# Key transposes of four heads at a time, rows doubled at read-out, in a cross-attention and expert-FFN kernel

## The reference

```
q = (layernorm(x) @ Wq + bq) in heads of 16
k = concat(side @ Wk + bk, ctx);  v = concat(side @ Wv + bv, ctx)
x = x + softmax(q k^T / 4) v @ Wp + bp
z = layernorm(x)
cw = softmax(z @ w_router) * softmax(z @ w_gating / 0.1);  cw /= sum(cw) + 1e-9
x = x + sum over 8 experts of cw[e] * ((silu(z @ w_gate[e]) * (z @ w_up[e])) @ w_down[e])
```

## Time and profile before

| what | value |
|---|---|
| median of 3 runs | 2790.26 us (2788.6 to 2790.9) |
| the profiled execution | 2790.06 us, of which its span is 2788.0 us |
| TensorE, VectorE, GpSimd, ScalarE busy | 98%, 79%, 65%, 61% of the span |
| granted TensorE clock, mean | 0.994 |
| HBM traffic | 89 GB/s over the span |

### The profile page before, as it was taken

The page is one execution under the profiler, slowest core; times in us unless marked ns, Lnnn a source line. Parts: engine busy times, 40 slices in busy tenths (PEclk is TensorE's granted clock), DMA queues, the critical chain, the costliest instruction groups (busy, mean ns, idle before and its releaser), DMA issues.

```text
span 2788.0 us, 47546 instructions
## 1 busy us (share of the span) xinstructions
PE 2723.0 (98%) x16416; PEld 2224.3 (80%) x16416; DVE 2189.3 (79%) x3254; ACT 1695.2 (61%) x3241; POOL 1813.8 (65%) x1886
## 2 busy tenths in 40 slices
PE   7789999999999999999999999999999999999998
PEld 5578878888887878878788787887878788888887
DVE  7877788778888788777787788877878778776665
ACT  7766666665666666566665666656666665544443
POOL 6766676666666667666676666766666666655554
PEclk9999999999999999999999999999999999999999
DMA  2113232332322323323222322323323233333332
GB/s 69 36 60 99 80 92 96 91 103 77 98 91 92 102 76 95 95 92 98 80 92 91 100 90 88 96 84 110 91 77 99 76 103 92 95 106 112 106 105 83
DMA packets 251275, 252.27 MB, mean 90 GB/s; under 512 B 15904, under 2 KB 242848, under 8 KB 251040
## 3 DMA queue, kind: packets, MB, share of 16 engines
q1 hardware_dynamic: 251040, 249.25, 28.8%
HBM read 240.66 MB, written 8.52 MB: 89 GB/s over the span
## 4 chain that ended last, share of the span: by engine, by line
PE 87%; DVE 7%; ACT 3%; issue 3%; POOL 1%; DMA 0%; POOLq 0%; ACTq 0%; DVEq 0%
PE ps_s L660 23%; PE ps_t L660 23%; PE ps_o L694 23%; PE ps_s L753 4%; PE ps_t L763 3%; PE ps_m L549 3%; PE ps_a L735 2%; PE ps_a L737 2%; DVE h_lo L949 2%; DVE negmax L1139 1%; PE ps_m L597 1%; PE ps_m L557 1%; DVE hf L944 1%; ACT h_hi L782 1%; DVE hf L937 1%
## 5 line engine op out<-in xcount | busy, mean ns | idle before, releaser
L949 DVE TENSOR_TENSOR h_lo<-hf,h_hi 128x512 fp32r<-128x512 f32 x512 | 506.0, 988 | 231.6 <-ACT h_hi L782 221.4
L782 ACT ACTIVATE h_hi<-hf 128x512 fp32r<-128x512 f32 x512 | 323.9, 633 | 510.6 <-DVE hf L944 510.6
L937 DVE SCALAR_TENSOR_TENSOR hf<-hf,ps_s 128x512 f32<-128x512 f32 x512 | 349.8, 683 | 278.0 <-ACT hf L777 275.2
L777 ACT ACTIVATE hf<-ps_s 128x512 f32<-128x512 f32 x512 | 305.6, 597 | 312.4 <-PE ps_s L660 204.5
L1170 POOL TENSOR_TENSOR wg_lo<-stage_w,wg_hi 128x512 fp32r<-128x512 f32 x256 | 340.0, 1328 | 224.1 <-ACT wg_hi L789 223.9
L1235 POOL TENSOR_TENSOR Pt_lo<-Pt 128x512 f16<-128x512 f32 x256 | 312.3, 1220 | 149.0 <-ACT Pt L916 148.5
L694 PE MATMUL ps_o<-h_hi,wd_hi 128*128 128x512 f32 x1024 | 399.9, 390 | 0.9 <-DVE h_lo L949 0.9
L694 PE MATMUL ps_o<-h_lo,wd_hi 128*128 128x512 f32 x1024 | 400.1, 391 | 0.0
L694 PE MATMUL ps_o<-h_hi,wd_lo 128*128 128x512 f32 x1024 | 398.5, 389 | 0.0
L1170 POOL TENSOR_TENSOR wd_lo<-stage_w,wd_hi 128x512 fp32r<-128x512 f32 x256 | 332.5, 1299 | 82.5 <-ACT wd_hi L789 82.4
L916 ACT ACTIVATE Pt<-ps_t 128x512 f32<-128x512 f32 x512 | 304.5, 596 | 124.1 <-PE ps_t L763 120.3
(11 more groups left out here) (193 smaller groups left out, 5117.0 us busy)
## 6 DMA issues: line engine op xcount, KB each, us to landing
stage_w<-in_L_ffn_w_gate_dram SPq DMA_DIRECT2D x256, 256.0 KB, 2.7
stage_w<-in_L_ffn_w_up_dram SPq DMA_DIRECT2D x256, 256.0 KB, 2.8
stage_w<-in_L_ffn_w_down_dram SPq DMA_DIRECT2D x256, 256.0 KB, 2.7
...
```

The source lines that it names most:

```text
L777: act.activation(hf[:], ps_g[:], ACT.Tanh, scale=0.5).then_inc(tanh_done, 1)
L782: act.activation(h_hi[f % FC][:], hf[:], ACT.Copy).then_inc(hh_done, 1)
L937: dve.scalar_tensor_tensor(out=hf[:], in0=hf[:], scalar=1.0, in1=ps_g[:], op0=ALU.add, op1=ALU.mult).then_inc(gate_done, 1)
L949: dve.tensor_tensor(h_lo[f % FC][:], hf[:], h_hi[f % FC][:].bitcast(F32), ALU.subtract).then_inc(hl_done, 1)
```

## The change

For batches 3 to 15 (`by_quad`) the eight items `kT` become four items `kQ`, at steps 12, 19 and 27 of the turn before and step 0 of its own. `kstack` is used as `qkeys`, with two slots a head (low, high), so that one transpose takes four heads: 4 x 2 x 16 = 128 columns. The doubling of the rows and the ones are made afterwards: `keys_out` on ScalarE copies, for each pair of heads, four blocks of 32 partitions (each head's low and high rows, twice) from PSUM to `KTs`, the first pair in the item's own program and the second in the next one; VectorE then sets 3 rows of ones in each head, two memsets of 3x512 in the program after each read-out. TensorE's score block waits for the ones as well. ScalarE's copies into the stack are half as wide.

The router arithmetic goes over programs 19 to 22, `cwT` to step 24, `d_cw` to step 25, and the reading back of `cwb` three (and two) steps later. `o`, `kv`, `xT` and `y` move one to two steps earlier, and so do the stack copies (from programs 12, 13 to 10, 11).

```diff
-                self.qs_at, self.ks_at, self.ms_at = (10, 8, 5) if b == -1 else (18, 12, 13)
+                self.qs_at, self.ks_at, self.ms_at = (10, 8, 5) if b == -1 else (18, 10, 11)
...
-                 (6, "qq", 2, 0), (8, "o", 0, -1), (9, "kv", 0, 1), (10, "qq", 3, 0), (11, "kv", 1, 1), (13, "xT", 0, 1),
+                 (6, "qq", 2, 0), (7, "o", 0, -1), (8, "kv", 0, 1), (9, "kv", 1, 1), (10, "qq", 3, 0), (11, "xT", 0, 1),
...
-                 (20, "kT", 1, 1), (21, "cwT", 0, -1), (22, "qq", 6, 0), (23, "y", 0, 0), (24, "y", 1, 0), (25, "kT", 2, 1),
-                 (26, "qq", 7, 0), (27, "kT", 3, 1), (28, "kT", 4, 1), (30, "qq", 0, 1)]
+                 (20, "kT", 1, 1), (21, "y", 0, 0), (22, "qq", 6, 0), (23, "y", 1, 0), (24, "cwT", 0, -1), (25, "kT", 2, 1),
+                 (26, "qq", 7, 0), (27, "kT", 3, 1), (28, "kT", 4, 1), (30, "qq", 0, 1),
+                 (0, "kQ", 3, 0), (12, "kQ", 0, 1), (19, "kQ", 1, 1), (27, "kQ", 2, 1)]
...
+            def keys_out(turn, ps, pair, d):
+
+                turn.wait(act, t_ps, d - 1, 4 * pair + 4)
+                for h in range(2):
+                    for part in range(2):
+                        src = 2 * HD * (pair % 2 * 2 + h)
+                        dst = HS * h + 2 * HD * part
+                        act.activation(KTs[dst:dst + 2 * HD, pair, :], ps[src:src + 2 * HD, :], ACT.Copy).then_inc(kT_done, 1)
...
+                    if name == "kQ":
+                        turn.wait(act, kT_ps, d, 2 * k + 2)
+                        keys_out(turn, ps, 2 * k, d)
+                    if keys_next:
+                        keys_out(turn, bank(keys_next[3]), 2 * keys_next[1] + 1, keys_next[2])
+                    keys_next = items[turn.b, step] if name == "kQ" else None
...
+                if step == 20:
                     turn.wait(dve, lsum_done, -1, 1)
                     dve.scalar_tensor_tensor(out=css[:], in0=lsum[:, :, 0], scalar=CW_EPS, in1=lsum[:, :, 1],
...
-                if step == 20:
+                if step == 21:
                     turn.wait(dve, csum_done, -1, 2)
...
+                if step == 22:
                     turn.wait(dve, crec_done, -1, 1)
...
+                            for h in range(2):
+                                ones = slice(HS * h + 2 * HD, HS * h + 2 * HD + 3)
+                                dve.memset(KTs[ones, pair, :].bitcast(F32), 1.0).then_inc(ones_done, 1)
```

More of the change, by code:

```diff
@@ L57, in bass_xattn_moe_ffn_kernel @@
     DVE_LOW = (1, 3, 5, 7)
+    QUADS = PAIRS // 2
+    FIRST_QUAD = 3
     SCALE = float(HD) ** -0.5
@@ L290, in q_ahead, with by_quad, keys_done @@
             return (k + 2) % PAIRS, d + (k + 2) // PAIRS
+        def by_quad(b):
+            return b >= FIRST_QUAD
+        def keys_done(b, pairs):
+            late = max(b - FIRST_QUAD, 0)
+            return (b - late) * PAIRS + late * 2 * QT * PAIRS + pairs * (2 * QT if by_quad(b) else 1)
         def released(b, name, k, d):
             turn = Turn(b)
+            if name in ("kT", "kQ"):
+                if not turn.has(d) or by_quad(b + d) != (name == "kQ"):
+                    return []
+                return [(kT_done, keys_done(b + d, 2 * k + 2 if name == "kQ" else k + 1))]
             if name == "y":
@@ L468, in body @@
                         eng.dma_start(x1_v[:, bass.ds((turn.b - 1) * QT, QT), :], X1[:]).then_inc(x1_out.sem, 16)
-                    if step == 22 and turn.has(-1):
+                    if step == 25 and turn.has(-1):
                         turn.wait(eng, cwT_done, -1, 1)
@@ L599, in do_misc @@
                     mm.then_inc(kT_ps.sem, 1)
+                elif name == "kQ":
+                    if k == 0:
+                        for count in (ks_h, ks_l, ms_h, ms_l):
+                            turn.wait(pe, count, 1, 1)
+                    for t in range(KC):
+                        mm = pe.transpose(ps[:, t * P:(t + 1) * P].bitcast(F32R), quad_block(t, k), ident_r[:])
+                    mm.then_inc(kT_ps.sem, 2)
                 elif name == "qq":
@@ L748, in body @@
                         if i % 4 == 0:
-                            turn.wait(pe, kT_done, d, h // 2 + 1)
+                            pe.wait_ge(kT_done, keys_done(turn.b + d, h // 2 + 1))
+                            if by_quad(turn.b + d):
+                                pe.wait_ge(ones_done, 2 * ((turn.b + d - FIRST_QUAD) * PAIRS + h // 2 + 1))
                             turn.wait(pe, qT_done, d, 2 * (h // 2) + 2)
@@ L842, in body @@
                         turn.wait(act, kT_ps, 0, PAIRS)
-                        act.activation(slots(kstack, 0, 0, 4, 3), heads_twice(KF), ACT.Copy).then_inc(ks_h.sem, 1)
+                        if by_quad(turn.b + 1):
+                            act.activation(qkeys[:, 0:QT * H, 1, :], heads(KF), ACT.Copy).then_inc(ks_h.sem, 1)
+                        else:
+                            act.activation(slots(kstack, 0, 0, 4, 3), heads_twice(KF), ACT.Copy).then_inc(ks_h.sem, 1)
                     if step == turn.ms_at and turn.has(1):
@@ L846, in body @@
                         turn.wait(act, kT_ps, 0, PAIRS)
-                        act.activation(slots(kstack, QT, 0, 4, 3), heads_twice(VF[:, QT:KC, :]),
-                                       ACT.Copy).then_inc(ms_h.sem, 1)
+                        if by_quad(turn.b + 1):
+                            act.activation(qkeys[:, QT * H:KC * H, 1, :], heads(VF[:, QT:KC, :]),
+                                           ACT.Copy).then_inc(ms_h.sem, 1)
+                        else:
+                            act.activation(slots(kstack, QT, 0, 4, 3), heads_twice(VF[:, QT:KC, :]),
+                                           ACT.Copy).then_inc(ms_h.sem, 1)
                     for o, at, d in v_at(turn):
@@ L1070, in body @@
                     router_weights(turn, step)
+                    for later in range(1, 3):
+                        name, k, d, _, _ = misc(turn, step - later)
+                        if name == "kQ":
+                            pair = 2 * k + later - 1
+                            dve.wait_ge(kT_done, keys_done(turn.b + d, pair + 1))
+                            for h in range(2):
+                                ones = slice(HS * h + 2 * HD, HS * h + 2 * HD + 3)
+                                dve.memset(KTs[ones, pair, :].bitcast(F32), 1.0).then_inc(ones_done, 1)
                     d, i = item_at(step, -1)
@@ L1251, in body @@
                         turn.wait(pool, ks_h, 1, 1)
-                        pool.tensor_tensor(slots(kstack, 0, 1, 2, 1)[:, :, 0, :], heads(KF),
-                                           slots(kstack, 0, 0, 1, 1)[:, :, 0, :].bitcast(F32),
-                                           ALU.subtract).then_inc(ks_l.sem, 1)
+                        lo, hi = (qkeys[:, 0:QT * H, n, :] if by_quad(turn.b + 1) else slots(kstack, 0, 1 - n, 2 - n, 1)[:, :, 0, :]
+                                  for n in range(2))
+                        pool.tensor_tensor(lo, heads(KF), hi.bitcast(F32), ALU.subtract).then_inc(ks_l.sem, 1)
                     if step == turn.ms_at and turn.has(1):
                         turn.wait(pool, ms_h, 1, 1)
-                        pool.tensor_tensor(slots(kstack, QT, 1, 2, 1)[:, :, 0, :], heads(VF[:, QT:KC, :]),
-                                           slots(kstack, QT, 0, 1, 1)[:, :, 0, :].bitcast(F32),
-                                           ALU.subtract).then_inc(ms_l.sem, 1)
+                        lo, hi = (qkeys[:, QT * H:KC * H, n, :] if by_quad(turn.b + 1) else slots(kstack, QT, 1 - n, 2 - n, 1)[:, :, 0, :]
+                                  for n in range(2))
+                        pool.tensor_tensor(lo, heads(VF[:, QT:KC, :]), hi.bitcast(F32), ALU.subtract).then_inc(ms_l.sem, 1)
                     f = turn.f(step)
```

15 lines of the change are left out of this document (10 added, 5 removed).

## The result

The changed kernel takes **2891.38 us**, median of 5 runs (2890.81 to 2896.22), against 2789.17 for the kernel before beside it: ratio 1.0367, 95% interval 1.0355 to 1.0379. It is slower, which was the likelier side of the forecast, but by 102 us instead of 19, and outside the range. The profile that follows is of the longest of the five executions, 2896.22 us; it is 106 us above the profiled execution of the kernel before.

A forecast was written before the change was run, and what follows sets the result against it. TensorE's stream was taken to set the time, and VectorE where it makes TensorE wait. Terms -14.0 + 8.4 - 3.6 - 1.9 + 16.9 + 13.0 = +18.8 on 2790.06 gave 2809 us; 8-in-10 range 2765 to 2840.

The forecast's parts named there:

- item at step 12: VectorE's programs 13 and 14 run late: 0.6 and 0.1 us lost, together 0.7 in 12 turns, +8.4 us.
- router and item at step 19: Steps 20 to 24, router arithmetic spread: -0.3 us a turn with removed transposes, -3.6 us; step 21 alone -0.76.
- item at step 27: VectorE's programs 28 and 29 run late: 0.5 and 0.8 us lost, together 1.3 in 13 turns, +16.9 us.
- item at step 0: VectorE's program 2 ends at 5.24 us against 4.2 allowed; over 13 turns +13.0 us.
- What the change takes off TensorE.: 52 key transpose items fewer at 0.36 us, 18.7 us; 39 stand by themselves, -14.0, the rest counted in the router.
- rival 4: Transposes don't leave TensorE's path, since it would only wait longer elsewhere; no chance of its own given.
- ScalarE's copies at 0.48 us: Each 512-column read-out into `KTs` takes 0.48 us, upper end 0.60; alone the copies stay hidden but use up slack.
- 1.2 us for a pair of memsets: VectorE's two memsets of ones cost 0.60 us each in eight programs a batch; other end 0.66 a pair.
- I leave each such delay as the row of before has it.: VectorE's two-SBUF-input instructions held up by GpSimd, like `cden` at 1.25 us, keep the delays of the earlier profile.
- the rule for a VectorE program: A VectorE program without rest lasts 3.32 us plus its extras plus what `h_lo` is held up.
- Rival 3: VectorE meets one more 1.3 us GpSimd instruction in two of the four places: 31 us, 2840 us; chance 0.12.
- rival 1: Short memsets absorbed by VectorE, or normalisations in programs 13 and 29 meeting a free GpSimd: 2767 us; chance 0.36.

The follow-up runs named there:

- the light GpSimd: Changed kernel with GpSimd's low parts of the expert weights at half their columns from the third unit on: 2829.40 us; same edit on the kernel before: 2763.72.
- the dummies: Kernel before plus two unread 3x512 scratch memsets in the programs where the changed kernel has its own: 2853.09 us; 2779.54 with GpSimd's weight work halved.
- the first experiment: Changed kernel with the four-head transposes switched off for all batches, all moves and the router's spread kept: 2794.39 us, ratio 1.0016.
- the cheap read-out: Changed kernel with one 128x512 copy a pair of heads instead of four, and no memsets of ones or wait for them: 2789.05 us, ratio 0.9994.

## Why the prediction was wrong in size

The side was right, and the reason for it: TensorE's transposes went, VectorE and ScalarE took the work over, and TensorE waits for `negmax` in the steps that were named. In us a turn, means of the turns 3 to 14:

| part | forecast | measured |
|---|---|---|
| three transposes gone | -1.1 | -1.1 |
| item at step 12 | +0.7 | +2.5 |
| router and item at step 19 | -0.3 | +1.5 |
| item at step 27 | +1.3 | +2.1 |
| item at step 0 | +1.0 | +2.8 |
| a turn | +1.6 | +7.8 |

Of the router's +1.5, 0.7 is the clock in step 22.

The twelve turns make 93 us of the profiled execution's 106, and 11 us more lie ahead of turn 3 (239.6 to 251.0), where the forecast had one or two.

The forecast's working can be laid beside the trace, since it says when VectorE starts a program and how long that lasts. A program is taken from its L990 to the next one's; us, means of the same turns:

| program | start into its step: forecast, measured | length: forecast, measured |
|---|---|---|
| 13 | 3.0, 4.22 | 7.14, 5.70 |
| 14 | 5.54, 4.87 | 5.13, 6.49 |
| 20 | | 5.86, 7.35 |
| 28 | 3.0, 3.24 | 5.94, 6.25 |
| 29 | 4.34, 4.89 | 6.51, 6.39 |
| 2 | 4.0, 4.72 | 6.99, 7.13 |

- **"What the change takes off TensorE."** Right in the steps concerned: step 1 is 4.60 for 4.96, step 4 4.66, step 28 4.59. Of the gain of 18.7 us the kernel without the memsets and copies kept 5.3. So rival 4, for which I saw nothing, was partly true: TensorE waited longer elsewhere in the turn.
- **ScalarE's copies at 0.48 us.** Mis-sized: 0.61, just over the upper end of 0.60. "Hidden, but it uses up the slack" failed too; they cost 30.6 us. They are why the programs 13 and 2 start late: with one copy instead of four the starts are 2.97 and 3.77. For step 3 the late start is 0.7 of the 0.9 us that are missing. In step 21 they put `Pt` off, GpSimd waits 0.78 for it, and VectorE stands behind GpSimd.
- **1.2 us for a pair of memsets.** It was 1.40: in the kernel with the light GpSimd `h_lo` costs 0.61 us from its start to the next instruction's, and 2.01 to that of the instruction behind the memsets, as 0.16 us of idle time stands before each. The forecast's other estimate, 0.53 us plus the start, lies above the row, which is 0.485; what counts in the stream is 0.65. At 0.2 us in eight programs that is at most 1.6 us a turn, some 20 of the 82 that are missing, and less where a program has rest.
- **"I leave each such delay as the row of before has it."** This is the step that failed most. Delays behind GpSimd aren't a property of an instruction but of where it falls. In program 20, 1.49 us longer than forecast, 1.09 is `css`, which took 1.24 us in place of `cden`'s 1.25, and 0.26 is `Pt_lo` with 0.94 for 0.68; so -0.76 for step 21 became +0.83. In program 14, 1.36 longer, `h_lo` and `Pt_lo` have 1.16 of delay where the forecast had none. In the programs 2, 28 and 29 the delays carried over were about right, and in 13, where the normalisations met a free GpSimd, they were 1.7 us too long. So the rule for a VectorE program was good, as the dummies show too, and its inputs weren't. Rival 3 named the mechanism; it counted two places and 31 us. With the light GpSimd step 21 is 5.78 for a forecast of 5.86, but that is luck: there `h_lo` has no delay where the forecast had 0.53, the pair takes 1.40 for 1.20, and VectorE waits 0.2 for tanh.
- **The steps behind.** Late programs went on past the steps that were priced: step 5 is 0.65 us longer, step 6 0.10 and step 31 0.33, which the forecast had at nothing.
- **Moved items at nothing.** In the turns this is true for `o`, `kv`, `xT` and `y`: the steps 7 to 13 of the first experiment sum to as much as before, 37.8 us. It isn't for the stack's low part, which meets `h_lo` in step 12. Ahead of turn 3 the profiled execution of the first experiment lost 5.4 us, while the router's spread alone lost none. But with the same moves and the cheap read-out only 1.0 was lost, so the moves alone don't explain it, and this is one execution of each, of kernels whose executions scatter by 9 to 13 us. The mean granted clock over the first 180 us was 0.91 in the kernel before, 0.89 in the first experiment and 0.88 in the changed kernel, and 0.92 in the kernel with the router on GpSimd, which was 2.6 us ahead there; what is cause and what effect stays open.
- **The clock** had no term. It took 8.7 us in the turns 3 to 14 of the profiled execution.
- **The normalisation** of rival 1 came true in program 13 (0.73 for 2.48 us) and not in program 29. It would have saved 1.7 us where the forecast lost 0.7, but `h_lo` and `Pt_lo` of the next program took it back.

The sum closes thus: 73.6 us for the memsets, 30.6 for the copies, -5.3 for the transposes and 4.4 for the moves are 103, against 102 measured. By mechanism it doesn't close as well: 36 us go with half of GpSimd's weight work, 9 of them the clock's, and how the other 66 divide between delays that were left, the length of VectorE's and ScalarE's streams, and the start of the kernel is open.
